# A convolution reordered by image, channels and half: matrices loaded once for two halves, patch-column input, transfers in line, three bank pairs

## The reference

```python
h = jnp.einsum('oc,bchw->bohw', w1, x)           # 48 -> 288 channels
h = jax.nn.relu(_bn(h, g1, b1, m1, v1))
h = jax.lax.conv_general_dilated(h, wd, padding=((1, 1), (1, 1)), feature_group_count=HID, ...)  # 3x3 per channel
h = jax.nn.relu(_bn(h, gd, bd, md, vd))
h = jnp.einsum('oc,bchw->bohw', w2, h)           # 288 -> 48 channels
return x + _bn(h, g2, b2, m2, v2)
```

## Time and profile before

| | |
|---|---|
| device time, median of 3 runs | 1933.91 us (1924.66 to 1934.29) |
| profiled execution | 1929.11 us, span 1927.3 us |
| TensorE matmuls busy | 1783.9 us, 93% of the span |
| VectorE, ScalarE, GpSimd busy | 1446.4, 1091.0, 418.4 us |
| HBM to and from the core | 206.94 MB, 286,893 DMA packets, 225,927 of them under 512 bytes |

### The profile page before, as it was taken

The page is one execution under the profiler, slowest core; times in us unless marked ns, Lnnn a source line. Parts: engine busy times, 40 slices in busy tenths (PEclk is TensorE's granted clock), DMA queues, the critical chain, the costliest instruction groups (busy, mean ns, idle before and its releaser), DMA issues.

```text
span 1927.3 us, 75807 instructions
## 1 busy us (share of the span) xinstructions
PE 1783.9 (93%) x30728; PEld 1410.8 (73%) x30728; DVE 1446.4 (75%) x2570; ACT 1091.0 (57%) x2550; POOL 418.4 (22%) x804
## 2 busy tenths in 40 slices
PE   5999999999999998799999888998988898999987
PEld 4888888888888886455555777777767777877765
DVE  4999999999999998566667566565656566666655
ACT  2888888888888886455555533343434343434432
POOL 4333333333333332502200440010101010101000
PEclk9999999999999999799999999899999999999989
DMA  1222222222222221677765566635545445545441
GB/s 66 70 73 78 73 78 74 76 74 77 74 77 75 76 76 63 164 185 175 169 151 139 154 149 160 139 80 128 125 110 124 115 98 136 112 112 132 101 119 39
DMA packets 286893, 206.94 MB, mean 107 GB/s; under 512 B 225927, under 2 KB 275560, under 8 KB 276840
## 3 DMA queue, kind: packets, MB, share of 16 engines
q1 hardware_dynamic: 282562, 197.37, 40.1%
q0 software_dynamic: 2400, 6.42, 1.6%
q10 hardware_dynamic: 1750, 0.39, 0.1%
HBM read 128.54 MB, written 62.98 MB: 99 GB/s over the span
## 4 chain that ended last, share of the span: by engine, by line
PE 48%; DMA 4%; issue 4%; ACT 3%; DVE 0%; SPq 0%; POOL 0%; DVEq 0%; ACTq 0%
PE psum L1183 14%; PE psum L1161 14%; PE psum L1219 6%; PE psum L684 5%; PE psum L665 3%; PE psum L655 3%; ACT h L896 3%; DMA piece<-img_mid 2%; PE psum L670 2%; DMA mats<-in_taps 1%; DMA room<-tok_mid 1%; DMA scaled_taps<-mats 1%; DMA room<-in_ident 0%; ACT room L754 0%; DVE yc L1306 0%
## 5 line engine op out<-in xcount | busy, mean ns | idle before, releaser
L1161 PE MATMUL psum<-ew,xp 64*100 64x96 f32 x6144 | 333.4, 259 | 41.6 <-ACT h L896 20.8
L1161 PEld LDWEIGHTS psum<-ew,xp 64*100 64x100 f32 x6144 | 306.3, 171 | 81.9 <-issue 39.6
L896 ACT ACTIVATE h<-psum 100x384 f32<-100x384 f32 x456 | 208.5, 490 | 255.9 <-PE psum L1161 255.9
L1183 PEld LDWEIGHTS psum<-h,mats 101*64 101x64 f32 x9216 | 287.8, 144 | 67.0 <-issue 66.6
L1183 PE MATMUL psum<-h,mats 101*64 101x64 f32 x9216 | 293.6, 228 | 45.8 <-issue 45.1
L896 ACT ACTIVATE room<-psum 128x512 f32<-128x512 f32 x216 | 129.0, 597 | 245.5 <-PE psum L1183 245.5
L897 DVE TENSOR_SCALAR h<-psum 100x384 f32<-100x384 f32 x312 | 173.4, 556 | 114.6 <-PE psum L1161 103.6
L348 PE MATMUL psum<-kb,qa 128*64 128x256 f32 x2048 | 243.7, 380 | 0.8 <-DVE prob L447 0.8
L935 POOL COPY xp<-piece 128x400 f32<-128x400 f32 x128 | 67.6, 528 | 651.9 <-DMA piece<-img_mid 651.6
L348 PEld LDWEIGHTS psum<-kb,qa 128*64 128x64 f32 x2048 | 140.6, 137 | 56.0 <-issue 1.5
L1284 DVE STREAM_TRANSPOSE room<-room 128x1024 f32<-128x1024 f32 x144 | 173.2, 1229 | 7.9 <-DVE room L897 0.5
(11 more groups left out here) (150 smaller groups left out, 2812.3 us busy)
## 6 DMA issues: line engine op xcount, KB each, us to landing
mats<-scaled_taps SPq DMA_DIRECT2D x63, 896.0 KB, 6.8
tok_mid<-mid SPq DMA_DIRECT2D x128, 224.0 KB, 1.9
room<-tok_mid SPq DMA_DIRECT2D x64, 448.0 KB, 4.4
piece<-img_mid SPq DMA_DIRECT2D x196, 63.8 KB, 2.4
img_mid<-room SPq DMA_DIRECT2D x128, 97.5 KB, 3.2
kb<-kk SPq DMA_DIRECT2D x512, 24.0 KB
scratch<-in_x_tokens SPq DMA_DIRECT2D x126, 96.0 KB, 2.0
out<-yc SPq DMA_DIRECT2D x14, 768.0 KB, 8.6
```

The lines of the kernel that those rows point to most:

```text
L896: return nc.scalar.activation(dst, src, ACT.Relu)
L1161: mm = nc.tensor.matmul(ring[(2 * J + u) % 4][0:PIN, p:4 * CH:4], xp[hx][rows, 4 * J + p, :], w1[rows, c, :], start=True, stop=True)
L1183: mm = nc.tensor.matmul(psum[POUT * u:POUT * u + POUT, BANK_OF[d] + n // 8, at:at + 4 * (PATCHES // 2) - n % 4:4], mats[ch // TCH][0:PIN + ...
```

## The change

- *Order.* Chunks go image, channels, half (`place`): `hx` changes fastest, so one load of `mats` serves two chunks. `yc` and `xp` exist once per half. From the second image on, an image's pieces are loaded while the third channel group of the image before is worked on.
- *Transfers.* `load_mats` runs after the whole filter of the second half is issued, and each load is waited for before the next is issued; output stores (now four of half the size per half) likewise. Matrices are still scaled and kept in the first image.
- *Input.* `img_mid` is laid out as four column groups of 34 columns with their borders, so a piece (16 rows now, 8 per half) is one contiguous run per channel. `xp` holds columns of patches, 130 rows x 10 pixels, so that rows are no longer copied twice; a patch is 100 contiguous elements of it. GpSimd cuts each piece with two copies of 48 lanes. Zero borders and lanes of ones are set once.
- *MLP output.* VectorE adds four border columns per strip in four small instructions; the two stores per strip are contiguous over 8 rows x 34 columns.
- *Banks.* The expansion rotates over three pairs (banks 0 to 5), restarting at J = 8: J waits for J-3, J = 8 and 9 for J-2, and J = 10 (whose banks 4 and 5 hold sums of the projection) for the first two additions. The projections wait for the evacuation of J = 5 or J = 13.

```diff
-        y = [sb(f"y{s}", [P, WS, GW + 2]) for s in range(2)]
+        y = [sb(f"y{s}", [P, 2, WS, GW // 2 + 2]) for s in range(2)]
...
+                    for to, c, column, lanes, of, at, x in ((slice(0, P), 0, end, slice(0, P), 1, 0, 0),
+                                                            (slice(0, P), 1, 0, slice(0, P), 0, n, WS - 1),
+                                                            (low, 1, end, high, 0, 0, 0),
+                                                            (high, 0, 0, low, 1, n, WS - 1)):
+                        nc.vector.tensor_tensor(y[1 - s][to, c, :, column], sums[of][lanes, at, :, x], held[of][lanes, at, :, x],
+                                                ALU.add)
...
-        piece = [sb(f"piece{s}", [P, PH + 2, SIDE]) for s in range(SLOTS)]
-        xp = [sb(f"xp{s}", [P, PATCHES // 2, PIN]) for s in range(2)]
+        piece = [sb(f"piece{s}", [P, ROWS, SIDE]) for s in range(2)]
+        xp = [sb(f"xp{s}", [P, PC // 2, H + 2, PW + 2]) for s in range(2)]
...
-        ring = [psum[:, s, :] for s in range(4)]
+        ring = [psum[:, s, :] for s in range(6)]
...
+        def place(k):
+            image, at = divmod(k, 2 * CHUNKS)
+            return image, at // 2, at % 2
...
+        def load_piece(eng, image, hx, j):
+            i = PIECES * (2 * image + hx) + j
+            wait(eng, cut, 2 * (i - 1))
             for r in range(2):
+                eng.dma_start(piece[i % 2][ONE * r:ONE * r + C, :, :].rearrange("c y x -> c (y x)"),
+                              d["img_images"][2 * hx + r, :, image, SIDE * ROWS * j:SIDE * ROWS * (j + 1)])\
+                    .then_inc(landed(i)[0], 16)
...
+            def store(image, hx, n):
+                k = 2 * CHUNKS * (image + 1) - 2 + hx
+                sp.wait_ge(y_done, added(k, n, GROUPS4 - 1))
                 for r in range(2):
...
+                    sp.wait_ge(y_stored[hx], 16 * (4 * image + 2 * n + r + 1))
...
+            def load_mats(m):
+                source = d["taps"] if m < CHUNKS else d["scaled_taps"]
+                for s in range(LOADS):
+                    if m <= CHUNKS:
+                        sp.wait_ge(mats_kept[s], 16 * m)
+                    sp.dma_start(mats[s][0:MROWS, :, :], source[LOADS * (m % CHUNKS) + s]).then_inc(mats_loaded[s], 16)
+                    sp.wait_ge(mats_loaded[s], 16 * m)
+
+            def chunk(k, last):
+                image, c, hx = place(k)
+                if hx == 0 and k < 2 * CHUNKS:
+                    keep_mats(c)
+                if c == CHUNKS - 1 and image + 1 < B:
+                    sp.wait_ge(unit_ready, ready_expand(k, PAIRS_E - 1, 1))
+                    wait(sp, y_done, added(k - 1, NSTEP - 1, GROUPS4 - 1))
+                    for j in range(PIECES):
+                        load_piece(sp, image + 1, hx, j)
+                if not last and (hx or image and c == 0):
+                    sp.wait_ge(unit_ready, ready_filter(k, DEPTHS - 1, DPARTS - 1))
+                if not last and hx:
+                    load_mats(k // 2 + 1)
+                for n in range(NSTEP):
+                    if hx and c == CHUNKS - 1:
+                        store(image, 0, n)
+                    elif image and hx == c == 0:
+                        store(image - 1, 1, n)
...
             def bank_free(k, J, u):
-                if J >= 2:
+                if J in (8, 9):
                     pe.wait_ge(*expands_done(k, J - 2, u))
+                elif J == 10 and k:
+                    if u == 0:
+                        pe.wait_ge(y_done, added(k - 1, 0, 1))
+                elif J == 10:
+                    pe.wait_ge(*expands_done(k, 5, u))
+                elif J >= 3:
+                    pe.wait_ge(*expands_done(k, J - 3, u))
...
+                    if not last:
+                        for u in range(2):
+                            pe.wait_ge(*expands_done(k + 1, 8 * n + 5, u))
```

More of the change, by code:

```diff
@@ L823, in conv @@
         assert sum(SEGMENTS) == PAIRS_E and len(SEGMENTS) == NSTEP
[L825 to L849, removed]
+        CONSTANTS = 2 + 5 + 1
+        FIXED = CONSTANTS + 2 + 6
         ACT_ALONE = (0, 8, 10)
@@ L955, in scale_mats @@
[L955 to L967, removed]
+        def scale_mats(pool, m):
+            for s in range(LOADS):
+                pool.wait_ge(*((mats_loaded[s], 16 * m) if m else (mats_begun[s], 16)))
+                at = CH * m + TCH * s
+                t = mats[s][0:MROWS, :, :]
+                nc.gpsimd.tensor_tensor(t, t, bc(scale[0:MROWS, at:at + TCH], 2, POUT), ALU.mult).then_inc(mats_scaled, 1)
+                pool.wait_ge(mats_scaled, LOADS * m + s + 1)
@@ new lines, in cut_piece @@
+        def cut_piece(pool, image, hx, j):
+            i = PIECES * (2 * image + hx) + j
+            pool.wait_ge(*landed(i))
+            src = piece[i % 2][:, :, :]
+            src = bass.AP(src.tensor, src.offset, [list(src.ap[0]), [PW, PC // 2], [SIDE, ROWS], [1, PW + 2]])
+            for r in range(2):
+                lanes = slice(ONE * r, ONE * r + C)
+                nc.gpsimd.tensor_copy(xp[hx][lanes, :, 1 + ROWS * j:1 + ROWS * (j + 1), :], src[lanes]).then_inc(cut, 1)
+                pool.wait_ge(cut, 2 * i + r + 1)
@@ new lines, in _ @@
+            assert len(constants) == CONSTANTS
+            constants += [(t[...], 0.0) for t in xp]
+            for hx in range(2):
+                for r in range(2):
+                    lanes = slice(ONE * r + 32, ONE * r + 64)
+                    constants.append((xp[hx][lanes, :, 1:H + 1, :], 1.0))
+                    if hx == r:
+                        edge = (PC // 2 - 1, PW + 1) if hx else (0, 0)
+                        constants.append((xp[hx][lanes, edge[0], 1:H + 1, edge[1]], 0.0))
@@ L979, in _, with put @@
+            assert len(constants) == FIXED
+            def put(first, last):
+                for n in range(first, last):
+                    t, value = constants[n]
+                    nc.gpsimd.memset(t, value).then_inc(fixed, 1)
+                    pool.wait_ge(fixed, n + 1)
+            put(0, CONSTANTS)
             loads = [(ident[:, :], d["ident"]), (w1[0:C, :, :], d["w1T"]), (w1[ONE:ONE + C, :, :], d["w1T"])]
@@ L1133, in chunk @@
                 if last:
                     for n in range(NSTEP):
[L1135 to L1137 removed]
+                        store(image, 1, n)
             schedule(sp, lambda: None, chunk)
[L1140 removed]
+            for hx in range(2):
+                sp.wait_ge(y_stored[hx], 64 * B)
         @block.tensor
@@ L1152, in bank_free, with expand @@
                     pe.wait_ge(unit_dve, dve_filtered(k - 1, 2 + J))
-            def expand(k, c, hx, J):
+            def expand(k, J):
+                image, c, hx = place(k)
+                if c == 0 and J == 0:
+                    pe.wait_ge(cut, 2 * PIECES * (2 * image + hx + 1))
                 for u in range(2):
@@ L1192, in first, with chunk @@
                 pe.wait_ge(mlp_done, STRIPS)
-                pe.wait_ge(border_set, 2)
+                pe.wait_ge(fixed, FIXED)
                 for J in range(PAIRS_E):
-                    expand(0, 0, 0, J)
+                    expand(0, J)
                 depthwise(0, 0)
-            def chunk(b, hx, c, last):
-                k = number(b, hx, c)
+            def chunk(k, last):
+                c = place(k)[1]
                 for u in range(1, DEPTHS):
                     depthwise(k, u)
-                if not last and c == CHUNKS - 1:
-                    pe.wait_ge(border_set, 2 * (2 * b + hx + 2))
                 def project(n):
@@ L1285, in turn, with add @@
                                     turned_patches(h2[:, :, BLK * e:BLK * (e + 1)], half)).then_inc(turned, 1)
-            def add(n, g, b, hx, c, k, last):
+            def add(k, n, g, last):
+                image, c, hx = place(k)
                 if g == 0:
```

214 lines of the change are left out of this document (67 added, 147 removed).

## The result

The changed kernel took 1820.0 us (median of 4 runs, 1816.24 to 1823.5), before 1929.29 (4 runs). The ratio is 0.9438, 95% interval 0.9392 to 0.9483: 5.6% faster. The forecast was 1841, range 1815 to 1889. The profiled execution is one of the four: 1823.5 us, span 1821.7.

A forecast was written before the change was run, and what follows sets the result against it. TensorE was taken to bound both stages, losing 92 us in the convolution to issue waits and clock. 1927.3 - 110.7 - 2.7 + 14.2 + 3 + 7.5 + 0.7, plus 1.8 around the span: 1841 us, range 1815 to 1889.

The forecast's parts named there:

- the prediction's own signs: Convolution on TensorE: among others, chunks of 30 to 31 us and a wait for the additions of under 0.5 us.
- Code waits: Convolution: issue waits, read as late code, fall from 61.5 to 9.5 us; +14.2 us left with the clock.
- why the waits would go: Convolution: loads in line and issued after the filter, with fewer loads, stores in line and longer runs, leave 9.5 us.
- Bank pairs: Expansion: three waits per chunk (1.0 us) go, a new wait for two additions costs 0.15 us per chunk.
- Image changes: An image's first chunk: additions wait about 1 us for stores at each of three images, +3 us (0 to 7).
- Tail: End of the kernel: four last stores run one after the other, +7.5 us (4.3 to 10.3).
- Small additions: Transformer's second half, VectorE: 0.65 us for four per strip, hidden except after the last strip, +0.7 us (0.3 to 1.3).
- GpSimd: First image: more copying (18.7 us) and clearing (at most 41 us) before scaling matrices, hidden, so nothing added.
- The first chunk: Convolution's first chunk: loses 0.9 us of issue waits and about 2 of evacuation waits, -2.7 us.
- half late: Rival: a single transfer still holds code up, 46 instead of 14 us of code waits, 1873 us; chance 0.16.
- issue waits stay: Rival: the convolution's issue waits are not code behind data and stay, 1919 us; chance 0.09.
- the third rival: Matrices late: loads in line delay the filter, using up the gain at 11.9 us a set; slower, chance 0.05.

## Why the prediction was right, and where its sizes were off

The direction and the stage were right, and so was the reading of the issue waits as late code; 1820 lies in the range, 21 us under the forecast. That it lies so near is in part luck: two terms missed widely and in part cancel, as the gain of the bank pairs was forecast 36 us too small and the loss at image changes 15 us too small. Two of the prediction's own signs failed with them: clean chunks take 28.7 us, not 30 to 31, and the wait for additions is 4.0 to 4.3 us at image changes, not under 0.5. By the prediction's own terms:

- *Code waits.* 9.5 us of issue waits were forecast: 6 beside the write-outs of scaled matrices and 1.1 at each image change, 14.2 with the clock. Beside the write-outs they are 7.2 us, and the chunks there lost 11.5 with the clock where 9 were forecast; one chunk after an image change lost 1.6, and no image change has a code wait. So the size was about right, and the restarts 1.3 to 1.7 us after a packet of code bear out that code was late. (The longest wait of before is 6.5 us, at 1836, not the 6.3 that I called the longest.) The step that said *why the waits would go* was not right: the line of transfers and the move into the expansion. Undone one by one or together they leave 6 to 21 us; place helped at image changes, where SP's order and not this edit set it. Two parts have a large effect in the kernel before: half as many loads (62 to 46 us alone) and stores cut to an eighth (62 to 30), both together 11. In the new order the line still takes 21 us of issue waits to 10, and pays for it with waits for the stores; in the old one it starved the pieces.
- *Bank pairs.* This term was mis-sized: 1.0 - 0.15 us per chunk were forecast, 19 us in 22 chunks; it is 31.17 - 28.67 = 2.5 us, 55. I took the 30.15 us of matmul rows of a clean chunk as work that has to be done. The round trip of a pair was in them: from the start of a J to that of the J two later it took 1.70 us, where the matmuls of two J take 1.41. On average a record took 52 ns between the waits that were shown, and takes 46 now. The new wait for two additions was forecast at 0.15 us and shows as at most 0.25 (6.14 us or 6.00 against 5.89 for the half with it). Undoing the edit gave 31.13 us, so this cause is shown.
- *Image changes.* Forecast 1 us of waiting for stores, and 1.1 us of code with its clock, at each: 8 in all. Measured 23.2. The chain was right in order and each link a little long: at the one shown, SP was free 9.7 us after the filter instead of 7.7, three loads took 16.7 us instead of 15.9, and a chunk of 28.7 instead of 30.3 us brought the additions 1.6 us earlier. The stores ended 43.1 us after the filter instead of 40.8, and a wait that was to be 1 us became 4.0, plus 1.3 for the third load, plus the clock. A faster chunk tightens every chain that has to fit into it; I had not carried the one term over into the other.
- *Tail* +7.5 forecast, +7.3 measured. *Small additions* 0.65 us per strip forecast, 0.61 measured, hidden but for 1.6 us in two of the last strips. With the wait before the first expansion, 1.72 instead of 1.14 us, the convolution began 1.9 us later, where 0.7 were forecast. *GpSimd* delayed nothing.

The first chunk gained 6.7 us where 2.7 were forecast, which is again the pace of the expansion. In sum 1927.3 - 109.9 (22 chunks) - 6.7 + 7.3 + 1.9 (start of the convolution) + 1.8 (last chunk, whose last projections ran at a lower clock, 0.72 granted from 1797 to 1803) = 1821.7, the span.

Of the rivals, "half late" and "issue waits stay" are refuted by 9.9 us of issue waits. The Trainium skill's rule in "Runtime: NRT & Kernel Launch", Instruction fetch mechanics, that crossing a block of code is mostly hidden, is borne out in the clean chunks: the one from 1752.47 to 1781.10 shows no issue wait while five packets of code land in it. It does not hold where large stores or several loads fly, with 62.4 us of issue waits in before. Matrices were late, as the third rival had it, by 0.6 to 1.5 us at image changes alone.

What stays open: the 0.8 to 4.5 us of code waits beside the write-outs of scaled matrices were not tried by themselves, and neither was a version that moves only the stores of an image change ahead of its pieces. Nor does a run part what spared the changed kernel the waits behind stores: it stores at three image changes and the end instead of at seven half ends and the end, mostly not inside a filter, and its stores go in packets of 4,096 bytes where before had 16,384.

## What to carry to other kernels

A matmul row that looks busy can hide a wait: compare the starts of single records between stretches with and without a dependence on an evacuation. Where the round trip of a buffer (here 1.70 us) is longer than the work that the other buffers give (1.41), a third buffer is worth more than the waits that the profile names. When "issue" waits come with bulk transfers, look at the code queue's packets, and at which transfers are in flight when none comes; cut bytes, or start them where code lasts longer. Putting everything in line costs its own waits. When several terms shorten the same chunk, work the chains that must fit into it out again with the shorter chunk.

## What the runs showed of the hardware

The expansion's records started 44 ns apart with two bank pairs and with three, at a granted clock of 1.00. With two, stops of 0.05 and 0.24 us by turns behind every 16 records, which the matmul rows do not show, made it 52 ns on average, against 46. In before TensorE restarted from its issue waits 1.3 to 1.7 us after a code packet had landed. In before code waits were as long as 6.5 us beside 1.5 MB of stores with matrices behind them; they were 5.0 us beside such stores with pieces alone, at most 3.2 us in the kernel with small stores, and up to 4.5 us beside the write-outs of matrices in the changed kernel. With single loads of 896 KB inside the filter 6.0 us of issue waits were left in the whole convolution. Cutting nine tenths of the 136-byte runs did nothing for them that shows.
